# Gated cross-attention with an expert layer on one core: edge tiles of the score matrix handled in halves of the head stacks, the second halves in the following unit

## The reference, cut to what matters

```python
scores0 = jnp.einsum('bhqd,bhkd->bhqk', qh, kh)
bias = jnp.einsum('bhqd,dr->bhqr', qh, p_params)
d = jnp.clip(jnp.arange(Ql)[:, None] - jnp.arange(Kl)[None, :], -MAX_DIST, MAX_DIST) + MAX_DIST
rel = bias[:, :, jnp.arange(Ql)[:, None], d]
scores = jnp.where(causal[None, None], scores0 + rel, NEG_INF)
attn = jax.nn.softmax(scores, axis=-1)
out = jnp.einsum('bhqk,bhkd->bhqd', attn, vh)
...
x = x + jnp.tanh(g_xattn[0]) * attention(ctx, layernorm(x))
x = x + jnp.tanh(g_ffn[0]) * experts(layernorm(x))
```

## Time and profile before

| | before |
|---|---|
| median of three runs | 665.16 us |
| the profiled execution, its own time | 667.02 us |
| its span, first to last instruction | 665.2 us |
| PE, PEld busy | 585.5 us (88%), 457.9 us (69%) |
| DVE, ACT, POOL busy | 427.2, 291.1, 196.5 us |
| idle PE until the transposes of line 997 may start | 17.1 us in 4 waits |

### The profile page before, as it was taken

The page is one execution under the profiler, slowest core; times in us unless marked ns, Lnnn a source line. Parts: engine busy times, 40 slices in busy tenths (PEclk is TensorE's granted clock), DMA queues, the critical chain, the costliest instruction groups (busy, mean ns, idle before and its releaser), DMA issues.

```text
span 665.2 us, 10536 instructions
## 1 busy us (share of the span) xinstructions
PE 585.5 (88%) x3256; PEld 457.9 (69%) x3256; DVE 427.2 (64%) x872; ACT 291.1 (44%) x549; POOL 196.5 (30%) x187
## 2 busy tenths in 40 slices
PE   4647988789879896978799999999999999999996
PEld 3525655456557563743678888888888888888885
DVE  5397658764887668764946747566475664756553
ACT  2444586446844594648424233242332423333221
POOL 4174035300560036100022332423223332333322
PEclk9777999899989899989989999999999999999999
DMA  5783435234442526262320220313102121021320
GB/s 177 174 201 94 97 69 158 57 93 89 109 105 72 123 53 152 71 217 52 83 74 27 92 68 13 100 47 94 64 18 93 47 96 64 30 82 48 96 65 32
DMA packets 43313, 58.13 MB, mean 87 GB/s; under 512 B 8368, under 2 KB 25520, under 8 KB 43248
## 3 DMA queue, kind: packets, MB, share of 16 engines
q1 hardware_dynamic: 42320, 56.16, 30.8%
q10 hardware_dynamic: 960, 1.57, 1.0%
HBM read 33.13 MB, written 6.11 MB: 59 GB/s over the span
## 4 chain that ended last, share of the span: by engine, by line
issue 50%; PE 22%; POOL 10%; DVE 10%; ACT 3%; DMA 2%; SPq 1%; ACTq 1%; POOLq 1%; DVEq 0%
POOL hl L1255 5%; PE oT L1018 3%; PE smax L953 3%; PE work L1033 2%; POOL d L458 2%; PE work L927 2%; PE oT L1022 2%; PE sT L998 2%; PE sT L997 2%; DVE mx L683 2%; DVE mx L711 2%; PE work L889 1%; SPq L339 1%; ACT ex L581 1%; DVE sx L698 1%
## 5 line engine op out<-in xcount | busy, mean ns | idle before, releaser
L1255 POOL TENSOR_TENSOR hl<-sg,hh 128x512 fp32r<-128x512 f32 x72 | 93.3, 1298 | 225.8 <-ACT hh L1300 225.8
L581 ACT ACTIVATE ex<-sT 128x512 f32<-128x512 f32 (+1 forms) x160 | 92.7, 594 | 93.0 <-PE sT L998 72.3
L1294 ACT ACTIVATE sg<-pg 128x512 f32<-128x512 f32 x72 | 43.2, 600 | 187.1 <-PE pu L1586 187.0
L1601 PE MATMUL py<-split,hh 128*128 128x256 f32 x576 | 115.3, 283 | 3.2 <-DVE x L1441 2.0
L683 DVE TENSOR_REDUCE mx<-smax 128x2 f32<-128x308 f32 x187 | 81.4, 473 | 30.7 <-PE smax L953 29.5
L1601 PEld LDWEIGHTS py<-split,hh 128*128 128x128 f32 x576 | 93.7, 189 | 9.5 <-DVE x L1441 4.4
L1586 PE MATMUL pu<-x2h,split 128*128 128x512 f32 x288 | 90.6, 396 | 0.0
L1586 PE MATMUL pg<-x2h,split 128*128 128x512 f32 x288 | 90.3, 394 | 0.0
L1601 PE MATMUL py<-split,hl 128*128 128x256 f32 x288 | 81.1, 282 | 0.0
L1429 DVE TENSOR_TENSOR sg<-cwb,sg 128x512 f32<-128x512 f32 x64 | 60.5, 947 | 11.0 <-DMA cwb<-cwt_d 8.2
L1586 PEld LDWEIGHTS pu<-x2h,split 128*128 128x128 f32 x288 | 54.1, 188 | 13.1
(11 more groups left out here) (163 smaller groups left out, 968.3 us busy)
## 6 DMA issues: line engine op xcount, KB each, us to landing
cwb<-cwt_d SPq DMA_DIRECT2D x64, 256.0 KB, 3.4
qs<-qh SPq DMA_DIRECT2D x56, 128.0 KB, 2.5
out<-x SPq DMA_DIRECT2D x8, 512.0 KB, 4.4
ks<-km SPq DMA_DIRECT2D x16, 231.0 KB, 3.5
qs<-ql SPq DMA_DIRECT2D x28, 128.0 KB, 2.5
at<-rden_d SPq DMA_DIRECT2D x56, 64.0 KB, 2.2
wx<-in_wx SPq DMA_DIRECT2D x9, 384.0 KB, 6.2
x<-in_x SPq DMA_DIRECT2D x3, 1024.0 KB, 13.7
```

Of the source, the lines that this page charges most:

```text
L581: nc.scalar.activation(ex[:, g % 2, i % 5, q0:HALF], ST[i % 2][:, q0:HALF], ACT.Exp).then_inc(exp_s, 1)
L1255: nc.gpsimd.tensor_tensor(hl[:, i % R, :], sg[:, i % R, :], hh[:, i % R, :], ALU.subtract).then_inc(hl_done, 1)
L1294: nc.scalar.activation(sg[:, i % R, :], PG[i % RG][:], ACT.Silu).then_inc(sg_s, 1)
L1601: last = nc.tensor.matmul(y, ha[:, i % R, q], wa[:, e, 2 * C * I:XW], start=(e == 0 and s == 0 and j % 2 == 0), stop=(e == NE1 - 1 and s = ...
```

## The change

The edge tiles are handled by halves of the eight stacks. The code that changes does this:

- POOL makes the table of tile 0 in two halves (of heads), and both tables before any subtraction. Its subtraction of tile 0 keeps only stacks 0 to 3 and comes when DVE has added the table of tile 1 (step 18). `tp` is made in two halves.
- The subtraction of stacks 4 to 7, of both tiles, is `late_stacks`: two instructions on POOL in the next unit (h = 0), behind `rstd` and the copies of the values. PE waits for them before step 10, and ACT before it overwrites `sx`.
- DVE takes add and maximum of tile 0 half by half (steps 10 and 11), and the maxima of tile 1 in halves, with the subtraction of stacks 0 to 3 between them.
- The prologue makes tile 1 first and tile 0 second, on PE, ACT, DVE and POOL.
- The reciprocals are taken at step 7 instead of 9, `keys_out` is issued behind the divisor loads, and unit 6 divides at steps 13 and 14.

```diff
     def first_tile(p):
-        return (p // (2 * NG)) + 2 * (p % 2)
+        return 1 - p // (2 * NG) + 2 * (p % 2)
...
+    def half_stacks(part):
+        return slice(part * NSTK // 2, (part + 1) * NSTK // 2)
...
         def divisors(u, h, new_keys=None):
-            if new_keys is not None:
-                keys_out(new_keys)
             sp.wait_ge(rden_s, u + 1)
             sp.dma_start(rden_d.rearrange("j (p n) -> (j p) n", p=32), dent[:]).then_inc(rden_out, 16)
...
             if new_keys is not None:
+                keys_out(new_keys)
                 keys_in(new_keys)
...
+        def tables(b, start):
+            for o, i in enumerate((1, 0) if start else (0, 1)):
+                pool.wait_ge(sx_s, 16 * b + 8 * (o + 1))
+                if o == 0 and not start:
+                    pool.wait_ge(sadd0_s, 4 * b)
+                    pool.wait_ge(sadd1_s, 3 * b)
...
+                for heads in ((slice(0, H // 2), slice(H // 2, H)) if i == 0 else (slice(0, H),)):
...
+        def whole_keys(i, part, done):
+            keys, largest = stacks(i, part)
+            nc.gpsimd.tensor_tensor(keys[:, :, :, 0:P], keys[:, :, :, 0:P],
+                                    largest.broadcast_to([P, NSTK // 2, 2, P]), ALU.subtract).then_inc(done, 1)
+
+        def early_stacks(b):
+            pool.wait_ge(sadd1_s, 3 * b + 1)
+            pool.wait_ge(sadd0_s, 4 * b + 2)
+            pool.nop().then_inc(waited, 1)
+            whole_keys(0, 0, sub0_s)
+            for part in range(2):
+                pool.wait_ge(sadd1_s, 3 * b + 2 + part)
...
+        def late_stacks(b):
+            pool.wait_ge(sadd0_s, 4 * (b + 1))
+            pool.nop().then_inc(waited, 1)
+            for i in range(2):
+                whole_keys(i, 1, late_s)
...
                 values(NW0 + NWORK * (b - 1) + V_USE)
+            if h == 0:
+                late_stacks(b)
             if h == 1 and ahead:
-                near(b + 1, False)
-                tile1_rest(b + 1)
+                tables(b + 1, False)
+                early_stacks(b + 1)
...
+        def tile0(b, part, start=False):
+            half = half_stacks(part)
+            keys = sx[:, 0, half, 0:PAIR].rearrange("p s (j k) -> p s j k", j=2)[:, :, :, 0:P]
+            dve.wait_ge(d_s, 4 * b + (3 if start else 1) + part)
+            nc.vector.tensor_tensor(keys, keys, by_stack(d0[:])[:, half], ALU.add).then_inc(sadd0_s, 1)
+            dve.wait_ge(sadd0_s, 4 * b + 2 * part + 1)
+            nc.vector.reduce_max(largest(0, half), keys, AX_X).then_inc(sadd0_s, 1)
...
-                if i == 9 and carry:
+                if i == 7 and carry:
                     reciprocals(u - 1)
-                if i in DIVIDE[h] and carry and ahead:
+                if i in DIVIDE[h] and carry and (ahead or h == 0):
...
                 if i == 19:
                     if diagonal:
-                        tile1(b + 1, 1)
-                        tile1(b + 1, 2)
-                    if h == 0 and not ahead:
-                        divide(u - 1, 1 - h)
+                        tile1_max(b + 1, 0)
+                        tile1_subtract(b + 1)
+                        tile1_max(b + 1, 1)
...
         max_out(0, 0, 9, start=True)
-        tile0(0, 0)
-        tile0(0, 1)
-        for part in range(3):
-            tile1(0, part)
+        tile1_max(0, 0)
+        tile1_subtract(0)
+        tile0(0, 0, True)
+        tile0(0, 1, True)
+        tile1_max(0, 1)
...
                 if step == 2 * 5:
+                    pe.wait_ge(late_s, 2 * (b + 1))
+                if step == 2 * 5 + 4:
                     pe.wait_ge(tp_s, 2 * (b + 1))
```

More of the change, by code:

```diff
@@ new lines, in tables, with stacks @@
+                if i == 1:
+                    pool.wait_ge(d_s, 4 * b + (1 if start else 3))
+                    nc.gpsimd.tensor_tensor(d1[:], d1[:], con("causal1").unsqueeze(1).broadcast_to([P, H, 32]),
+                                            ALU.add).then_inc(d_s, 1)
+        def stacks(i, part):
+            half = half_stacks(part)
+            keys = sx[:, i, half, 0:PAIR].rearrange("p s (j k) -> p s j k", j=2)
+            return keys, mx[:, i, :].rearrange("p (j s) -> p s j", j=2)[:, half].unsqueeze(3)
@@ L502, in gpsimd @@
         values(4)
-        near(0, True)
-        tile1_rest(0)
+        tables(0, True)
+        early_stacks(0)
         batches(pool, unit)
@@ L703, in tile1, with largest @@
[L703 to L716 removed]
+        def largest(i, half):
+            return mx[:, i, :].rearrange("p (j s) -> p s j", j=2)[:, half]
@@ new lines, in tile0, with tile1_add @@
+        def tile0(b, part, start=False):
+            half = half_stacks(part)
+            keys = sx[:, 0, half, 0:PAIR].rearrange("p s (j k) -> p s j k", j=2)[:, :, :, 0:P]
[3 more added lines that the diff above has]
+            nc.vector.reduce_max(largest(0, half), keys, AX_X).then_inc(sadd0_s, 1)
+        def tile1_add(b, start=False):
+            keys = sx[:, 1, :, 0:PAIR].rearrange("p s (j k) -> p s j k", j=2)
+            dve.wait_ge(d_s, 4 * b + (2 if start else 4))
+            nc.vector.tensor_tensor(keys[:, :, :, P - DIST:KL], keys[:, :, :, P - DIST:KL],
+                                    by_stack(d1[:, :, 0:K1 + DIST]), ALU.add).then_inc(sadd1_s, 1)
```

91 lines of the change are left out of this document (31 added, 60 removed).

## The result

| | after | against before |
|---|---|---|
| median | 664.19 us (661.79 to 667.11, 20 runs) | 668.12 us (663.96 to 674.09, 20 runs) in the same session |
| ratio | 0.9942 | 95% interval 0.9927 to 0.9957 |
| the profiled execution, its span | 663.06 us, 660.9 us | 667.0 us, 665.2 us |

The ratio times the 665.16 us of the forecast's scale is 661.3 us, 3.9 us less than before; the forecast was 662.1 us, 3.1 less. The small total hides large terms of both signs.

What follows compares the result with a forecast made beforehand. PE was taken to bound the kernel, hardly pausing in the experts and stopping in attention for late edge tiles or DVE. Terms 1.6 - 2.2 + 1.0 - 2.1 - 1.9 + 0.5 = -3.1 us took 665.16 to 662.1, range 660.1 to 664.1.

Steps and rivals of the forecast that it cites:

- The late subtractions hold the normalisations: Units 0, 2, 4: DVE's normalisations stand at least once per late POOL subtraction; within the +1.6 and +1.0 us terms.
- The first rival: Late subtractions hit nothing, or one normalisation slips in each time: -8 to -11 us, 655.5; chance 0.20.
- What the new wait at step 5 costs: Units 2 and 4: border gain lost, PE 0.5 us later at step 5; +0.5 each, +1.0 together.
- the third rival: Slower: new PE waits at step 5 may lower its clock, 1.3 us each time or more; 668.7, chance 0.10.
- The divisors: Units 2 and 4: earlier reciprocals and loads remove DVE's two waits for the divisors; -1.9 us.
- Units 1, 3 and 5: Steps 10 to 18: POOL's long subtraction leaves the divisions' steps; -0.75 us each, -2.2 for three.
- the borders' 6.3 us: Borders into units 2, 4 and 6: PE's wait before the transposes of `sx` goes, 6.3 us over three.
- The tails: Units 1, 3 and 5, late steps: divisions no longer held by POOL's long subtraction; -0.75 us allowed per unit.
- The table of tile 0 in halves brings nothing: Units 1, 3 and 5: POOL's second half holds DVE's add, so both orders end together; no gain.
- The prologue: Before unit 0: PE starts 1.3 us earlier; with unit 0's later normalisation wait the term is +1.6 us.
- Unit 6: Earlier division waits 2.4 us on DVE, PE loses about 3.1, the end loses its 2.31 wait; +0.5 us.
- The second rival: DVE's gains in units 1, 3, 5 miss PE and POOL wins every change of hands: 666.2 to 668.3; chance 0.18.

Runs made afterwards that it cites:

- experiment 1: Changed kernel, with POOL's two late subtractions waiting until all four normalisations are done in units 0, 2 and 4; 655.34 us, ratio 0.9795.
- experiment 4: Changed kernel plus ten extra matmuls on PE in front of its wait for the normalised x in units 0, 2 and 4; 663.99 us, ratio 0.993.
- experiment 7: Changed kernel with late subtractions behind the normalisation and unit 6 dividing at step 19, plus six extra matmuls at step 5 of units 2 and 4; 651.06 us, 0.9723.
- experiment 6: Kernel before the change with only the divisor edits: reciprocals at step 7, key stores behind the divisor loads; 664.82 us, ratio 0.9931.
- experiment 5: Changed kernel with reciprocals back at step 9 and key stores ahead of the divisors' store and loads; 671.17 us, ratio 1.0014.
- experiment 11: Changed kernel with the table of tile 0 made by one POOL instruction over all heads; 666.31 us, ratio 0.9957.
- experiment 8: Changed kernel with late subtractions behind the normalisation and unit 6 dividing at step 19, plus all four normalisations at step 4 where h = 0; 652.03 us, 0.974.
- experiment 2: Changed kernel with unit 6 dividing at step 19 again instead of steps 13 and 14; 663.32 us, ratio 0.9912.
- experiment 9: The edits of experiment 7 and experiment 8 together on their common parent: four normalisations at once and six extra matmuls; 651.38 us, ratio 0.9741.

## Why the prediction was right

The time came out 0.8 us from the forecast, but not for the forecast's sum: that the total fits so well is luck. By its steps:

- **The late subtractions hold the normalisations.** Right, and shown: experiment 1 moves only their place and gives back 9.8 us. Even the shape was right, one normalisation per subtraction, a second pair undisturbed in unit 0. The first rival, that they hit nothing, had a price of 655.5; the kernel in which they hit nothing is experiment 1, at 0.9795, or 651.5 on the forecast's scale. The rival's mechanism was not what happened, and its price was too modest.
- **What the new wait at step 5 costs.** Here the sum failed, in "for all the gain at the border PE is 0.5 later at step 5". It priced waits and kept the clock out; the clock stood as the third rival with 1.3 us each time and a chance of 0.10. The traces show 9.7 us given back in units 2 and 4 where 5.2 were forecast, and the clock low behind all three waits. The wait itself was priced about right: in unit 2 the transposes of x start 14.57 us behind the projection's start in both kernels, where 15.1 was forecast. Of the missing 4.5 us, 3.6 lie behind the transposes: from their start to step 10 it takes 11.01 us instead of 9.40 in unit 2, and 11.36 instead of 9.41 in unit 4. The other 0.9 lies ahead of them, in unit 4, where they start 14.73 us behind the projection's start instead of 13.09. Experiments 4 and 7 show that a change of the clock alone, at the same or more work, is worth 1.3 to 1.6 us in a unit. The third rival's mechanism was real. Its time did not come because the change also takes low clock away, behind the border into unit 2 (0.68 before from 119.7 to 125 us, 1.00 now from 118 to 121) and, which no rival names, behind step 15 of units 2 and 4.
- **The divisors.** Mis-sized by the same neglect, with the other sign: -1.9 forecast, -4.6 (0.9931, interval 0.9905 to 0.9957, or -6.3 to -2.9 us) alone in experiment 6 and -4.8 by experiment 5. The term was DVE's two waits. PE's wait at step 15 shrank from 2.49 to 1.04 us in unit 2 and from 1.64 to 1.04 in unit 4, 2.05 together, which is the term, and the low clock behind it went away too, 0.72 to 1.00 in the windows of both units.
- **Units 1, 3 and 5.** Of the borders' 6.3 us all but some 0.6 came as forecast (no wait is left above 0.3 us). The tails, from step 15 to the projection, brought 1.1 to 1.3 each where 0.75 were allowed. "The table of tile 0 in halves brings nothing" held within 0.2 us (experiment 11). The rest of the 2.5 us (11.0 against 8.5) is in the projections, 3.62, 3.63 and 3.63 us instead of 3.90, 4.27 and 3.88, and in steps 0 to 10 of units 3 and 5, 0.5 together. Why these got shorter is not shown.
- **The prologue.** PE began 2.6 us sooner in this pair of profiles, 1.3 were forecast. The old prologue began unit 0 at 54.79 and 53.13 us in its two profiles, the new one between 51.63 and 55.09 over the eleven with the same code there. The median of the eleven is 52.36. A single pair can't decide between 1.3 and 2.6. The loss behind it was larger too, 4.5 us: the transposes of x start 2.9 us later against the start of unit 0, as forecast, and the matmuls behind them take 1.6 us more, which was not in the sum. The net of +1.9 stands beside +1.6 because two terms grew alike.
- **Unit 6.** +0.9 for +0.5, and not by the steps that were priced. DVE waited 1.99 us for the last load where 2.4 were forecast, and PE 2.53 for 3.1; behind step 15 that is made up by the end of the unit, 13.67 us against 13.62. The loss is the wait of the reciprocals at their new place, which the sum put at nothing: steps 0 to 10 take 10.39 us in the changed kernel and 10.35 with the divisors' edits alone (experiment 6), and 9.63 before and without those edits (experiment 5).
- **The second rival**, that DVE's gains of units 1, 3 and 5 don't reach PE, is refused by the 11.0 us and by the tails in them.

The forecast of the total was right because two omissions, mostly of the clock, +4.5 in the give-back and -3.2 in the divisors, nearly cancelled, and units 1, 3 and 5 took the difference.

## What to carry to other kernels

When a POOL instruction is moved, look at which DVE instructions with two SBUF inputs or a `tensor_scalar` then lie under it, and who waits for them; here one semaphore wait in front of two subtractions was worth 9.8 us, more than twice what the whole change brought. The halves of the edge tiles, which the change is about, brought nothing measurable until that wait was in; the gain of the change as it was is that of the divisors. Price every wait on PE twice, as the time it stands alone and with the matmuls behind it at the low clock, and a wait that is removed the same way. The two are the ends of a range, since the same wait left the clock high in one execution and low in another. The version that took both to heart, with the subtractions behind the normalisation, one wait instead of two at step 5, matmuls to fill it and unit 6's division in DVE's idle time, runs at 0.9669 of the time before (0.9643 to 0.9695), against 0.9942 for the change as it was.

## What the runs showed of the hardware

- A wait's length did not settle what the clock did behind it. Behind 1.67 us it was 0.75 and 0.68 in unit 2 and 1.00 in unit 4 of one execution (experiment 8). In front of unit 6's projection a wait of 2.31 us left the 16 matmuls at 5.23 us before the change, one of 2.31 us left them at 3.72 in experiment 2, and one of 2.30 at 6.50 in experiment 6. In unit 4 waits of 1.05 and 0.62 us stood in front of the transposes of x in the kernel before and in experiment 6; from the transposes to step 10 it then took 9.41 and 10.56 us. What else enters was not isolated.
- Extra matmuls can make a unit shorter: six of them, 1.56 us of PE's time in experiment 9, bought 1.5 us each in units 2 and 4 (experiment 7). Where the clock was already low, ten of them cost 1.4 us (experiment 4).
- A GpSimd memset holds a `tensor_scalar` as a subtraction does. And the hand-over differs: at the change from one subtraction to the next a waiting normalisation got in (in unit 0 the two took 1685 and 1995 ns), at the change from one memset to the next none did (1589 ns for the first in unit 0, and 2491 in unit 4 under the multiplication of line 430 and both memsets, the next ones 0.40 us). At the change from line 430 to the first memset one got in in unit 2 (718 ns) and none in unit 4. What decides it is not shown.
